# Thirty products that nothing reads, ahead of the first expert's transposes

## What is computed

```python
h = jax.nn.relu(jnp.einsum('ecd,edf->ecf', dispatched, w1))   # 8 experts, 640 slots, 512 -> 2048
expert_out = jnp.einsum('ecf,efd->ecd', h, w2)                # 2048 -> 512
...
out = jnp.einsum('ks,ksm->sm', combine_weights, rerouted)     # back to the tokens, times the gate
```

## Time and profile before

| | |
|---|---|
| median of three runs | 1220.02 us |
| lowest, highest | 1217.79, 1220.59 us |
| the profiled execution | 1219.18 us |
| its span, first to last instruction | 1217.1 us |
| TensorE (PE) busy | 1039.4 us, 85% |
| VectorE (DVE), ScalarE (ACT), GpSimd (POOL) busy | 677.7, 533.8, 322.6 us |
| mean granted clock of TensorE | 0.953 |

### The profile page before, as it was taken

How to read it: one execution, slowest core, us unless ns; L and a number is a source line. 1 busy time by engine, 2 the same in 40 slices (tenths; PEclk the granted TensorE clock), 3 DMA queues, 4 the chain that set the end, 5 groups by cost and what they waited for, 6 DMA issues and landing times.

```text
span 1217.1 us, 17595 instructions
## 1 busy us (share of the span) xinstructions
PE 1039.4 (85%) x5058; PEld 827.9 (68%) x5059; DVE 677.7 (56%) x970; ACT 533.8 (44%) x914; POOL 322.6 (27%) x251
## 2 busy tenths in 40 slices
PE   1146797787799829999999999999999999999994
PEld 0022344344348529998999899989898888999883
DVE  6989899899781523334333433355555344343553
ACT  5455746826844212334333433344545334333453
POOL 3878818648630330001100200020201101100302
PEclk9998998997999759999999999999999999999998
DMA  5251340211010452113421621282535234322711
GB/s 191 104 166 35 122 133 35 69 70 69 0 71 35 174 175 104 69 69 118 106 69 69 149 76 69 69 220 91 186 138 186 83 132 134 87 69 69 216 70 21
DMA packets 63406, 125.29 MB, mean 103 GB/s; under 512 B 4726, under 2 KB 4762, under 8 KB 63384
## 3 DMA queue, kind: packets, MB, share of 16 engines
q1 hardware_dynamic: 54728, 107.91, 25.6%
q0 software_dynamic: 8656, 17.13, 7.0%
HBM read 93.04 MB, written 35.22 MB: 105 GB/s over the span
## 4 chain that ended last, share of the span: by engine, by line
PE 58%; issue 1%; ACT 1%; DVEq 1%; DVE 1%; POOL 0%; ACTq 0%; POOLq 0%
PE ps_y L1137 10%; PE ps_y L1138 10%; PE ps_y L1139 10%; PE ps_h L1117 9%; PE ps_h L1119 9%; PE ps_h L1118 9%; PE ps_t L1087 1%; POOL out_dram L1066 0%; ACT xh L1232 0%; ACT y L1239 0%; DVEq L1177 0%; DVE hl L1294 0%; ACT w1h L1204 0%; DVE w1l L1255 0%; ACTq L1177 0%
## 5 line engine op out<-in xcount | busy, mean ns | idle before, releaser
L1117 PE MATMUL ps_h<-xh,w1h 128*128 128x320 f32 (+3 forms) x768 | 247.6, 322 | 7.9 <-issue 4.0
L1119 PE MATMUL ps_h<-xh,w1l 128*128 128x320 f32 (+3 forms) x768 | 243.6, 317 | 0.0
L1118 PE MATMUL ps_h<-xl,w1h 128*128 128x320 f32 (+3 forms) x768 | 243.5, 317 | 0.0
L1066 POOL DMA_INDIRECT out_dram<-y,token x40 | 64.6, 1615 | 657.6 <-ACT y L1239 487.7
L1294 DVE SCALAR_TENSOR_TENSOR hl<-ps_h,hh 128x320 fp32r<-128x320 f32 (+1 forms) x192 | 106.9, 558 | 194.0 <-ACT hh L1228 185.3
L1137 PE MATMUL ps_y<-w2h,hh 128*128 128x512 f32 x528 | 206.5, 391 | 1.9 <-DVE hl L1294 1.9
L1138 PE MATMUL ps_y<-w2h,hl 128*128 128x512 f32 x528 | 206.7, 391 | 0.0
L1139 PE MATMUL ps_y<-w2l,hh 128*128 128x512 f32 x528 | 206.1, 390 | 0.0
L1258 DVE TENSOR_TENSOR w2l<-raw,w2h 128x512 fp32r<-128x512 f32 x128 | 88.6, 692 | 196.5 <-ACT w2h L1207 193.6
L1228 ACT ACTIVATE hh<-ps_h 128x320 fp32r<-128x320 f32 (+1 forms) x192 | 94.4, 492 | 232.4 <-PE ps_h L1119 232.2
L1207 ACT ACTIVATE w2h<-raw 128x512 fp32r x128 | 80.7, 631 | 211.2 <-PE ps_y L1139 210.2
(11 more groups left out here) (194 smaller groups left out, 1290.4 us busy)
## 6 DMA issues: line engine op xcount, KB each, us to landing
raw<-in_L_ffn_w_dram SPq DMA_DIRECT2D x64, 1024.0 KB
slots<-r_rows SPq DMA_DIRECT2D x8, 1302.5 KB, 16.1
rows<-slots SPq DMA_DIRECT2D x8, 1302.5 KB
f_rows<-in_fside_BxSxS_dram SPq DMA_DIRECT2D x5, 1024.0 KB, 5.3
rows<-in_x_dram SPq DMA_DIRECT2D x4, 1024.0 KB, 6.4
out_dram<-x_rows SPq DMA_DIRECT2D x4, 1024.0 KB, 4.9
slots<-r_rows POOLq DMA_DIRECT2D x1, 1302.5 KB
rows<-slots SPq DMA_DIRECT2D x5, 260.5 KB, 4.1
```

The costliest lines, as they stand in the source:

```text
L1117: nc.tensor.matmul(o, w1h[:, j, dt, :], xh[:, dt, lo:hi], start=(dt == 0), stop=False)
L1118: nc.tensor.matmul(o, w1h[:, j, dt, :], xl[:, dt, lo:hi], start=False, stop=False)
L1119: last = nc.tensor.matmul(o, w1l[:, j, dt, :], xh[:, dt, lo:hi], start=False, stop=(dt == CT - 1))
```

## The change

Five lines stand between TensorE's first instruction in the second block (a semaphore increment) and the transposes of the first rows. TensorE waits for the high parts of the first weights and then issues 30 products, each 128x128 times 128x512 in fp32r, into the bank `ps_t`. Each of them starts and ends its own sum, so each overwrites the last; nothing reads the bank before a turn inside an expert has written it. The stationary operand goes through the four 128x128 parts of `w1h[:, 0]`, the moving one is always `w2h[:, 0]`.

```diff
         pe.sem_inc(s_f, 2)
+
+        pe.wait_ge(s_wh1, 1)
+        pe.wait_ge(s_wh2, 1)
+        for n in range(30):
+            nc.tensor.matmul(ps_t[:].rearrange("p t q -> p (t q)"), w1h[:, 0, n % CT], w2h[:, 0], start=True, stop=True)
         for i in range(ST):
             first_turn(i)
         with pe.Fori(0, NE) as e:
```

## The result

The changed kernel takes 1226.23 us (median of six runs, 1223.41 to 1227.37) against 1218.53 (1217.45 to 1220.59) in six runs of the kernel before. The ratio is 1.0055, 95% interval 1.0044 to 1.0065: slower by 6.7 us, between 5.4 and 7.9. The forecast was 1225.4, in a range of 1222.4 to 1228.3.

The account below looks back on a forecast made before the run. TensorE's dense expert stream bounds the kernel, so a delayed start reaches the end: 1219.18 + 6.1 (delay) - 0.65 (clock) = 1224.6 us, or 1225.4 on the runs' median, which is 0.84 higher; range 1222.4 to 1228.3.

Parts of the forecast that it names:

- The border: End of the first block, near 447.1 us: all engines leave together, and the products start at 447.2 to 447.4, not before.
- That they could hide ahead of it: Rival: products run in TensorE's idle time before the border and cost nothing; 1220.02 down to 1217.3 us; chance 0.03.
- The products' price: 30 products ahead of the transposes: 8 at half clock in 3.45 us, then 22 at full clock in 5.0 us.
- One sign: Over the whole kernel, TensorE's busy time was to be higher by 7 to 12 us.
- The chain behind them: Transposes, ScalarE's copy, VectorE's subtractions, then issue: 0.66 + 0.60 + 3.07 + 1.49 = 5.8 us to the first real product.
- The load of the next rows: SyncE's load, which waits for all transposes, goes out near 458 instead of 451.68; 7 us later costs nothing.
- The delay: First real product of the first expert starts at 461.6 instead of 455.46, 6.1 us later, passed on to the end.
- The clock: Ahead of the first expert, TensorE idles 3.6 us and its clock falls again, so the products' warming is lost.
- The term of 0.65 us given back: Expert stream's start: half clock for 4.2 us instead of 5.5, so 0.65 us come back, ends -0.2 and +1.1.
- The rival "the clock holds": Full clock lasts through the chain to 461.6, giving the stream back 2.75 us: 1223.4 us; chance 0.16.
- The Trainium skill's rule on transposes: Transposes don't count as clock activity; by it idleness begins at 455.75, "clock holds" is out, up to 0.4 us more.

Follow-up runs that it names:

- the 48: Against the kernel before: 48 products of the same kind at the end of TensorE's part of the first block, ahead of the border; 1218.13 us, ratio 0.9993.
- the kernel with the weights held back: Against the changed kernel: the second 2 MB of weights load only after the first half of the second up-projection; 1224.15 us, ratio to before 1.0047.
- with 15: Against the changed kernel: 15 products ahead of the transposes in place of 30; 1221.31 us, ratio to before 1.0022.
- with 60: Against the changed kernel: 60 products ahead of the transposes in place of 30; 1232.58 us, ratio to before 1.0112.
- the kernel with the waits alone: Against the changed kernel: its two waits stay, its 30 products go; 1219.75 us, ratio to before 0.9999.
- twenty: Against the kernel before: 20 products behind the transposes, ahead of the first expert; 1219.22 us, ratio 1.0000.
- with the weights held back too: Against the kernel before: ten products behind the transposes, and the second 2 MB of weights load after half the second up-projection; 1216.31 us, ratio 0.9979.

## Why the prediction was right

*The border.* Right. First product at 448.04, with the memsets; TensorE's own sequencer ends 15.90 us of idleness. They start 0.6 us later than the forecast's 447.2 to 447.4, as the whole border does. That they could hide ahead of it is excluded, and the 48 that were written ahead of it were free.

*The products' price.* Sized 8.45 us (8 at half clock, 22 at full), measured 8.44. It was partly luck: the clock rose 3.3 us after their start here, but after 4.0 in the kernel with the weights held back (8.79 us for thirty) and after 5.1 with 15 and with 60. One sign was missed: TensorE's busy time should have gone up by 7 to 12 us and went up by 5.9, since the transposes, at full clock, were busy 2.34 us and not 4.15.

*The chain behind them.* Sized 5.8 us from first transpose to first real product, measured 5.87, and 5.84 with sixty. VectorE's five subtractions bind it (3.08). The load of the next rows went out at 459.02 instead of 451.68 and cost nothing, as said.

*The delay.* 6.1 us forecast, 6.33 measured from the border; 6.41 at the second up-projection and 6.3 at the first turn. It reaches the end whole. Against the kernel with the waits alone it is 7.0, 7.3 and 7.2 us; the 6.7 of the times lies between.

*The clock.* The fall ahead of the first expert is as forecast. The term of 0.65 us given back was mis-sized for this execution: the clock rose 6.1 us after the first real product, not 4.2, and gave back nothing. In the six other kernels where it had fallen it rose 3.0 to 4.2 us after that product, in the kernel before 5.5; so the term is a matter of the single execution, and the 5.5 that the prediction set it against was a long one. Without that term the sum is 1220.0 + 6.1 = 1226.1, beside the measured 1226.23. The step itself was 6.7 where 5.4 was forecast; that the absolute time came closer is luck: the median of before came down to 1218.53 with more runs.

*The rival "the clock holds"* had the wrong price, and would have had it even if it had come true. It took the clock's whole 2.75 us as gained. The ten products behind the transposes are nearly that case: full clock from the first up-projection on, 2.7 us less for it, and the second up-projection 13.8 us after the border, against 14.6 in the kernel before and 13.7 with the waits alone; nothing in the time. The prediction took TensorE's clock as the only thing that sets the first up-projections, and in the profile of before no idle time lies between them. The other limit couldn't be seen there, since the slow products covered it. It is no limit everywhere: with thirty behind the transposes, where the first up-projection meets the end of the transfers (DMA share 0.27 from 458, then 0.00), first to second is 3.52 us at full clock.

*The Trainium skill's rule on transposes.* The Trainium skill, "TensorE: Matmul & The Clock Gate", Part 4 (PE-mode transpose), says that full clock doesn't engage for transposes in transpose mode. The kernel before and the one with the waits alone have nothing but the 20 transposes on TensorE there, and the clock rose 3.4 and 3.6 us after the first of them (447.33 to 450.76, 449.15 to 452.74); the profile doesn't say which mode they are in. If it is transpose mode, these traces disagree with the page. In the changed kernel it stayed full until 461.6, through 2.3 us of transposes and 2.8 of idleness. No experiment took the transposes away from the products, so whether they carried it on is not shown.

*Left open.* That the idle time ahead of the second up-projection is code being fetched is argued, not shown. The traces go further than the row "issue", though. Each has one packet of 0.02 MB on an instruction queue (q8) near the first up-projection; with ten products it lies between 457.0 and 457.5:

```profile
q8 instruction: 1, 0.02, 13.7%
```

Looked up to 0.1 us, this packet comes 2.4 to 3.3 us after the first real product in the five kernels whose first up-projection runs under full DMA engines (before, waits alone, 48, ten, twenty), and 0.2 to 0.6 us after it in those with the weights held back. The second up-projection starts in none of the thirteen traces less than 2.9 us after the packet, and 2.9 to 3.1 us after it in the four where TensorE idles. That fits code which comes late behind the transfers and which the second up-projection needs; whose packet it is the profile doesn't say. In the changed kernel the packet came at 464.1, so that a clock that held could have brought back some 1.6 us (468.69 - 464.15 - 2.9, an estimate) and not 2.75.

## What to carry to other kernels

Work that only keeps an engine warm has to stand in time in which that engine is idle for another reason: behind the last step that feeds the chain, not ahead of its first. "While the data are on their way" must be read from the timeline; here the border between the blocks had used up most of that time. And before a faster clock is priced, ask what the slow one covers: here it was a wait of up to 2.1 us ahead of the second up-projection, which appears only beside the transfers and is probably for code, and only warming and quiet together paid.

## What the runs showed of the hardware

With only transposes of 128x128 behind it, the granted clock went to full 3.4 us after their start in the kernel before. After 12.9 us of dense products it outlived 2.9 us of idleness and the first transposes, fell at 447.7 in the kernel with 48 (0.50 from 448 to 451), and rose once more at 451.1, when the transposes had ended. From the first to the second up-projection TensorE took 5.84 us with ten products (2.06 of it idle; DMA share 1.04 from 455 to 457, 0.08 from 459) and 3.62 with the weights held back too (0.03), both at full clock. The instruction packet near the first up-projection came 2.8 us after it in the first case and 0.3 in the second.
